# One gather column in three groups fetched row by row on SyncE, and six row buffers in all passes

## The reference, cut to what matters

```python
ke = k[src] + e;  score = sum(q[dst] * ke) / sqrt(...)        # conv, passes c1 and c2
a = exp(score - segment_max(score, dst)[dst])
out = segment_sum(a / denom[dst] * (v[src] + e), dst)
e = alpha_s[src] + alpha_d[dst] (+ edge term)                  # gat, passes c3, c4, c5
out = segment_sum(softmax(leaky(e)) * h[src], dst)
z = h[src] + h[dst] + ef                                       # pna, pass c6
agg = [segment mean, max, min, std of z over dst]
```

## Time and profile before

| | us |
|---|---|
| median of the runs | 13483.18 |
| span of the profiled execution | 13480.4 |
| POOL busy | 10010.5 (74%) |
| DVE busy | 6813.4 (51%) |
| ACT busy | 4134.7 (31%) |
| the six edge passes | about 1950 each |

### The profile page before, as it was taken

How to read it: one execution, slowest core, us unless ns; L and a number is a source line. 1 busy time by engine, 2 the same in 40 slices (tenths; PEclk the granted TensorE clock), 3 DMA queues, 4 the chain that set the end, 5 groups by cost and what they waited for, 6 DMA issues and landing times. The chain is left out here.

```text
span 13480.4 us, 46161 instructions
## 1 busy us (share of the span) xinstructions
PE 515.1 (4%) x1768; PEld 338.5 (3%) x1768; DVE 6813.4 (51%) x10542; ACT 4134.7 (31%) x4038; POOL 10010.5 (74%) x10585
## 2 busy tenths in 40 slices
PE   3000001100000300000010000000000000000001
PEld 1000000100000200000000000000000000000000
DVE  2787776477777433333333333343333335656566
ACT  4333333233333312222212222211111113666663
POOL 7777777777777677777777777777777776777775
PEclk9999999555555655555555555555555555555555
DMA  8444443344444222222212222222222222444443
GB/s 328 128 126 119 119 119 100 95 119 119 120 120 120 57 66 63 63 61 63 60 47 59 59 58 59 59 48 57 59 59 59 58 59 82 159 159 157 159 153 121
DMA packets 919562, 1312.58 MB, mean 97 GB/s; under 512 B 600892, under 2 KB 616404, under 8 KB 906113
## 3 DMA queue, kind: packets, MB, share of 16 engines
q0 software_dynamic: 341536, 381.76, 15.7%
q10 hardware_dynamic: 85680, 537.82, 10.2%
q1 hardware_dynamic: 492209, 391.76, 10.1%
HBM read 651.09 MB, written 659.48 MB: 97 GB/s over the span
## 5 line engine op out<-in xcount | busy, mean ns | idle before, releaser
L1767 POOL DMA_INDIRECT c_y<-g_tab,srcs x4689 | 4426.0, 944 | 1429.0 <-issue 1376.9
L2200 POOL DMA_INDIRECT c_y<-h_tab,srcs x1563 | 1474.8, 944 | 510.8 <-issue 466.5
L741 POOL DMA_INDIRECT c_y<-h_tab,srcs x1563 | 1474.9, 944 | 476.3 <-issue 476.3
L1796 DVE TENSOR_TENSOR c_s<-c_y,c_ad 128x64 f32<-128x64 f32 (+1 forms) x297 | 79.1, 266 | 3450.0 <-DMA c_y<-g_tab,srcs 3448.7
L741 POOL DMA_INDIRECT first_y<-h_tab,srcs x1483 | 1399.3, 944 | 452.9 <-issue 451.7
L1879 ACT ACTIVATE c_ex<-c_de 128x64 f32<-128x64 f32 (+1 forms) x297 | 67.4, 227 | 2321.1 <-DVE c_de L1827 2320.0
L1840 DVE TENSOR_TENSOR_SCAN c_acc<-c_r,c_w_in 128x1156 f32<-128x1156 f32 (+1 forms) x297 | 753.0, 2535 | 23.2
L763 DVE TENSOR_TENSOR_SCAN c_q_all<-c_mask,c_q_in 128x408 f32<-128x408 f32 (+2 forms) x792 | 734.0, 995 | 17.8 <-issue 10.5
L806 DVE TENSOR_TENSOR_SCAN c_acc<-c_r,c_w_in 128x408 f32<-128x408 f32 (+2 forms) x792 | 731.1, 986 | 8.2
L839 ACT ACTIVATE c_q_in<-c_q_raw 128x1552 f32<-128x1552 f32 (+1 forms) x198 | 596.2, 3011 | 195.8 <-DVE c_q_in L822 195.8
L1893 ACT ACTIVATE c_row<-c_acc 128x1088 f32<-128x1088 f32 (+1 forms) x297 | 617.7, 2080 | 0.0
(11 more groups left out here) (402 smaller groups left out, 6461.6 us busy)
## 6 DMA issues: line engine op xcount, KB each, us to landing
rows_d<-c_row ACTq DMA_DIRECT2D x97, 2048.0 KB, 6.9
rows_d<-c_row ACTq DMA_DIRECT2D x291, 576.0 KB, 2.9
rows_d<-c_row ACTq DMA_DIRECT2D x194, 784.0 KB, 3.4
c_q_raw<-q_start SPq DMA_DIRECT2D x194, 776.0 KB, 4.5
q_start<-first_y SPq DMA_DIRECT2D x97, 776.0 KB, 9.0
c_y<-g_tab,srcs POOLq DMA_INDIRECT x4689, 2.5
c_y<-h_tab,srcs POOLq DMA_INDIRECT x3126, 2.5
c_ea<-in_edge_attr SPq DMA_DIRECT2D x97, 512.0 KB
```

What stands on the lines that cost most here:

```text
L741: nc.gpsimd.indirect_dma_start(y[:, g % NY, k, 0:D], None, h_tab, source(g, k))\
L1767: nc.gpsimd.indirect_dma_start(y[:, b, k, :], None, g_tab, source(g, k))\
L2200: nc.gpsimd.indirect_dma_start(y[:, b, k, :], None, h_tab, source(g, k))\
```

## The change

Of every third group (the groups in row buffers 2 and 5, `SYNC_SLOTS`) column 15 is not gathered by POOL. SP fetches it with 128 DMAs of one row each, into one partition each. Their addresses are in registers: a table `places_d` in DRAM, made in `begin`, holds for each such column the 128 source numbers times the row's size in bytes; SP loads one row of it into SBUF (`at`, two rows) one run ahead, and fills 32 registers at a time with a TENSOR_LOAD. The class is written with three parts for the run; `THIRDS = [0, P, P, P]` puts all 128 rows in the first part. The run for buffer 5 stands behind the operands of group 6n + 1, the run for buffer 2 of the next round behind those of group 6n + 4. In c2 to c6 the first run stands ahead of the loop; in c1 POOL still gathers the first such column whole, in `begin`.

`y` has six buffers in `gat_edges` and `pna_edges` too, POOL waits for the group six before, and DVE's loop is unrolled over six groups instead of two. DVE waits for the rows of SP (`sync_got0`, `sync_got1`) besides those of POOL. In `begin` SP loads 32 columns of `src` (32x128 single words), DVE makes the table in three operations at the end of its list, and SP stores it.

```diff
+EVERY, SYNC_K = NY // 2, GW - 1
+SYNC_SLOTS, NSYNC = [EVERY - 1, NY - 1], NGRP // EVERY
+THIRDS = [0, P, P, P]
...
+def by_pool(g):
+    return width(g) - (g % NY in SYNC_SLOTS)
...
+        def third(self, sp, b, part):
+            lo, hi = THIRDS[part:part + 2]
+            rows = self.tab.rearrange("n f -> (n f)").bitcast(U8)
+            for a_, z in zip(range(lo, hi, 32), range(lo + 32, hi + 32, 32)):
+                _, places = nc.values_load_multi_w_load_instructions(
+                    self.at[b:b + 1, a_:z], [mybir.EngineType.SP], min_val=0, max_val=(NP_ - 1) * 4 * self.width,
...
+                for p, place in zip(range(a_, z), places):
+                    sp.dma_start(self.y[p:p + 1, SYNC_SLOTS[b], SYNC_K, 0:self.width].bitcast(U8),
+                                 rows[bass.ds(place, 4 * self.width)].rearrange("(a n) -> a n", a=1))\
+                        .then_inc(self.got[b].h, 16)
+
+        def work(self, sp, n, j, more=True):
+            if j == 0:
+                self.third(sp, 0, 2)
+            elif j < EVERY + 1:
+                if j == 1:
+                    self.await_places(sp, n, 1)
+                    if more:
+                        self.load_places(sp, n + 1, 0)
+                self.third(sp, 1, j - 1)
+            elif more:
+                if j == EVERY + 1:
+                    self.await_places(sp, n + 1, 0)
+                    self.load_places(sp, n + 1, 1)
+                self.third(sp, 0, j - EVERY - 1)
...
-                with sp.Fori(1, NGRP // NY) as n:
+                with sp.Fori(1, NGRP // NY - 1) as n:
                     for j in range(NY):
                         operands(n, j, GW)
+                        by_sync.work(sp, n, j)
...
-                    for k in range(width(g)):
+                    for k in range(by_pool(g)):
...
-        y = st.sb("y", [P, 2, GW, TG])
+        y = st.sb("y", [P, NY, GW, TG])
...
-                    if g >= 2:
-                        pool.wait_ge(*weighted[b](g // 2))
+                    if g >= NY:
+                        pool.wait_ge(*weighted[g % 2]((g - NY) // 2 + 1))
```

More of the change, by code:

```diff
@@ L360, in _ @@
                 sp.dma_start(prev_i[:], a["dst"][0:EP].rearrange("(p t) -> p t", p=P)).then_inc(dst_loaded.h, 16)
+                with nc.allow_non_contiguous_dma("one column of src in three groups"):
+                    sp.dma_start(src_i[:], a["src"].rearrange("(p t) -> t p", p=P)
+                                 [EVERY * GW - 1:EVERY * GW * NSYNC:EVERY * GW, :]).then_inc(src_loaded.h, 16)
                 sp.wait_ge(*zeroed(1))
@@ L1746, in _, with operands @@
                 sp.dma_start(ad_raw[:], by_edge(ad_start)).then_inc(ad_loaded.h, 16)
+                by_sync.begin(sp)
+                def operands(n, j, w, more=True):
+                    i, b = n * (NY // 2) + j // 2, j % 2
+                    if bd is not None:
+                        sp.wait_ge(*e_scored[b](i))
+                        edge_attrs(i, b, w)
+                    if w == GW:
+                        if j == 1 or j == EVERY + 1 and more:
+                            sp.wait_ge(*weighted[b](i))
+                        by_sync.work(sp, n, j, more)
                 if bd is not None:
@@ L1749, in _ @@
                         edge_attrs(0, b, GW)
[L1750 to L1753, removed]
+                by_sync.whole_first(sp)
+                by_sync.work(sp, 0, 1)
+                for j in range(2, NY):
+                    operands(0, j, GW)
+                with sp.Fori(1, NGRP // NY - 1) as n:
+                    for j in range(NY):
+                        operands(n, j, GW)
+                for j in range(NY):
+                    operands(NGRP // NY - 1, j, GW, False)
+                if bd is not None:
                     for b in range(2):
@@ L1862, in _ @@
                 v.wait_ge(*ready(3))
-                with v.Fori(0, HALF - 1) as i:
-                    for b in range(2):
-                        step(piece(i, b))
+                with v.Fori(0, NGRP // NY) as n:
+                    for j in range(NY):
+                        step(piece(n * (NY // 2) + j // 2, j % 2), j, n)
                 for pc in LASTS:
-                    step(pc)
+                    step(pc, pc.slot, NGRP // NY)
                 fix_on_vector(v)
@@ L2180, in edge_attrs, with operands @@
                                  [:, bass.ds((i * 2 + b) * GW, w), :]).then_inc(e_loaded[b].h, 16)
+                def operands(n, j, more=True):
+                    i, b = n * (NY // 2) + j // 2, j % 2
+                    sp.wait_ge(*added[b](i))
+                    edge_attrs(i, b, GW)
+                    by_sync.work(sp, n, j, more)
+                by_sync.begin(sp)
                 for b in range(2):
                     edge_attrs(0, b, GW)
[L2184 to L2187, removed]
+                by_sync.whole_first(sp)
+                by_sync.work(sp, 0, 1)
+                for j in range(2, NY):
+                    operands(0, j)
+                with sp.Fori(1, NGRP // NY - 1) as n:
+                    for j in range(NY):
+                        operands(n, j)
+                for j in range(NY):
+                    operands(NGRP // NY - 1, j, False)
                 for b in range(2):
```

109 lines of the change are left out of this document (81 added, 28 removed).

## The result

The changed kernel takes **14942.5 us** (14933.5 to 14945.0), where the kernel before took 13483.4 us beside it on the same chip: **1.108 times as long, 95% interval 1.106 to 1.110**. The prediction of 15,260 us was 2% too high, the direction and the range were right.

A forecast was written before the change was run, and what follows sets the result against it. POOL's gathers, 1.248 us each, were taken as the bound. Conv +1430, c3 +240, c6 +180, c4 and c5 -80, beginning +5 gave +1775 us on 13480.4: 15,260 us, range 13,600 to 16,700.

The forecast's parts named there:

- The loop: In each third group on SP: run, operands, their landing, ACT's turn, DVE up to `weighted`, next run; 82.6 us in conv.
- T: SP's run of 128 row DMAs at 0.41 us plus four register loads of 1.3 us: 57.7 us, ends 41.7 and about 65.
- The third rival: Each register filled by its own trip, so SP bounds all six passes: 76 us a run, 18,740 us; chance 0.10.
- The backlog: SP's queue held up behind the 128x16-piece edge DMA in conv passes: 3.0 us.
- Conv passes: In c1 and c2 three groups take 82.6 us instead of 59.9: +22.7 us a run, 63 runs, +1430 us.
- c3: Pass with edge attributes through PE: three groups take 67.4 us, +7.5 us a run, 32 runs, +240 us.
- c6: Pass with ACT's lift and DVE's sum: three groups take 65.6 us, +5.7 us a run, 32 runs, +180 us.
- or if the row DMAs slow other transfers: Last listed way for the prediction to be wrong: SP's row DMAs slow other transfers; no size given.
- c4 and c5: Passes without operands on SP: 58.5 us a run, just inside POOL's 58.7, so the gain is whole, -80 us.
- Six buffers: In gat and pna passes: POOL was never held up with two buffers, so four more give 0.
- The first rival: Run hidden if under about 34 us in conv, 0.26 us a row: faster, 13,250 us; chance 0.09.
- The second rival: About no change: a run of 37.5 us, conv loss against the other passes' gain, 13,480 us; chance 0.03.

The follow-up runs named there:

- e_thirds: The changed kernel with its run of 128 rows cut into pieces of 32, 64 and 32, each behind another group's operands: 13,791.4 us, ratio 1.023.

## Why the prediction was right, by its steps

**The loop** was right, and it is the cause. The predicted waits are there: ACT for `q_raw` once in three groups (33 us each, where some 20 were expected), POOL for DVE (1066 us in all in c1 and c2, where the kernel before has 1.2). Without the run, the loop was put at 24.9 us; measured 76.85 - 52.7 = 24.1.

**T**, the run with its register loads, was put too long, 57.7 us for a measured 52.7 (from 1549.7, where the table row's issue ends, to 1602.4, the end of the run). Two errors partly cancel. The rows and the loads of the changed kernel:

```profile
L312 SPq DMA_DIRECT2D c_y<-g_tab x12288: 224/225/849, 5927.7 to 12181.7; - x199
L312 SPq MOVE c_y<-h_tab x8192: 29/29/38, 3129.2 to 14650.8; - x200
...
L308 SPq TENSOR_LOAD <-c_at x764: 2026/2124/3279, 398.5 to 14638.2; - x191
```

A row lasts 0.225 us, less than any short DMA in the earlier trace rows, from which 0.34 was taken. The MOVE is there as predicted. Start to start it is (50.43 - 3 x 2.2) / 128 = 0.34 us, not 0.41, in quiet stretches 0.32: the lower bound was nearer. A load takes 2.12 us, not 1.3: between its bounds, near the upper one. The 5 us of T in 63 runs of the conv passes are 315 us, and the forecast was 317 us too high. That this is so neat is chance: the conv passes were put 272 us too high and c3 192, and c6 155 too low.

The Trainium skill ("Runtime: NRT & Kernel Launch", "Instruction fetch mechanics") has about 200 ns a register. The measurement of loads from SBUF differs: from 16 to 32 registers the load grows by 0.91 us, 57 ns a register. The third rival fell with it.

**The backlog** behind the edge DMA was put at 3.0 us. The table row's issue behind it takes 2.4 to 3.3 us, 2.7 in the median; in c4, where no edge DMA precedes, it takes 0.22.

**Conv passes**: +22.7 us a run were expected, 17.7 with the right T; the period grew by 17.2, and 18.4 were measured with what comes at the ends of the passes.

**c3**: +240 expected, +48 came. With T at 52.7 the sum is 62.4 and +2.5 us a run, 80 us; 61.2 us was its period in the trace. Right mechanism, T mis-sized.

**c6**: +180 expected, +335 came. Here the step that failed is "or if the row DMAs slow other transfers", put last among the doubts and with the wrong sign: the other transfers slow the row DMAs. The run of rows is 9.4 us longer than c4's 49.8, by the rows behind three stores; the period is 70 us where the sum had 65.6. That a shorter T and a slower c6 partly cancel is luck.

**c4 and c5**: -80 expected, -78 came. Runs of some 50 us lie inside 58.7, and the gain is whole.

**Six buffers**: 0, as the run with the buffers alone shows. But the prediction took them to be neutral in every case. Beside a late DVE six buffers move part of the loss behind the pass, where no view of the gathers sees it: 48 us of it in c3 and 93 in c6, whose buffers the change made six. That this adds nothing to the loss is read from the periods (+10 us a run in c6 are 320 of its 335 us); no kernel was run with two buffers beside the row DMAs.

**The first rival** put the limit of a hidden run at 33.8 us. A run of 64 rows, 27.6 us with its two loads, is hidden; one of 96 rows, some 40 us, costs 433 us. That brackets the limit as worked out. What the prediction did not have is a second limit behind it. Take the loop away, and SyncE's own work per three groups (run, table row, operands and the backlog) is 60 to 64 us against 58.7. It did say that SyncE would "just keep up" by itself; that left out the operands. The second rival's 13,480 us lies outside the stated range too, so what the prediction gave to the outside is 0.22 and not 0.19.

## What to carry to other kernels

Work moved from a busy queue to an idle one is free only if what stands behind it on that queue is not on somebody's path. Before a long run of issues is put into an in-order queue, add up the loop that goes through it, and then the queue's whole time per period; both must be under the bound's period, and cutting the run cures the first alone. Put loads with a deadline on another queue, and leave such a run out of a pass in which large stores are under way.

## What the runs showed of the hardware that was not expected

- A one-row DMA (256 or 288 bytes) with its address in a register is issued by SyncE in some 0.225 us, 0.32 us start to start with its MOVE. The shortest issue in the trace of before is 0.28 us.
- A load of registers from SBUF: 1.24 us for 16, 2.15 us for 32 in the rows above, so some 0.3 us and 57 ns for each register.
- While a store of 2 MB by ScalarE is on its way, SyncE's one-row DMAs take about 1.0 us each to issue, five of them for a store. With twice the bytes there are nearly twice as many of them (25.6 a run for 14.4); with packets of 4 KB for 16 KB still some two thirds (about 10).
- A register load can take much longer than 2.1 us. In e_thirds' c6 the loads took 5.2 us in the median, and those right behind a table row's DMA 6.9 to 7.3. An edge load of 512 KB stands in front of every piece, and a 2 MB store is under way in every group; no run tells which of the two it is:

```profile
L308 SPq TENSOR_LOAD <-c_at x36: 2052/5160/7292, 12606.3 to 13192.1; - x36
```
